# A fused decoder layer on one core: cross k and v and the expert bias from fp32r parts, and score rows stacked one head group at a time

## The chip, the cores and the metric

The kernel runs on 1 core of one Trainium2 chip. The metric is device microseconds (us) from launch to end; lower is better. The core has five engines that run side by side and meet only through semaphores: TensorE (PE in the profile, with its weight loads listed apart as PEld), VectorE (DVE), ScalarE (ACT), GpSimd (POOL) and SyncE (SP), which here only issues DMAs.

## The reference, cut to what matters

Batch B = 8, T = 512 tokens, D = 256. A linear attention with a decaying state comes first, then cross-attention to a context, then a block of self-attention plus a mixture of experts; a layernorm follows each.

```python
# cross-attention: 16 heads of 16
kh = proj(ctx, w_k, b_k); vh = proj(ctx, w_v, b_v); qh = proj(x, w_q, b_q)
out = softmax(qh @ kh.T / 4) @ vh;  x = layernorm(x + out @ w_o.T + b_o)
# third block
qkv = x @ W_qkv + b_qkv                      # self-attention, 16 heads of 16
gate = softmax(x @ W_gate + b_gate)          # 8 experts, the best two kept in `combine`
expert_out = einsum('bsd,edf->bsef', x, W_experts) + b_experts
moe_out = einsum('bsef,bse->bsf', expert_out, combine)
x = layernorm(x + attn_out + moe_out)
```

## The kernel before, in words

**The order is written out by hand.** For each batch n there is a cross phase C n and a self phase S n. They run as C0, C1, S0, C2, S1, ..., C7, S6, S7: 16 phases of 4 head groups (four heads each), and each group takes 4 **slots**, one for each block of 128 keys. So there are 256 slots, and every slot has two halves, h = 0 and h = 1. All engines walk through the same list of halves, t = 2*slot + h, from slot -23 (the prologue) to the end. A table entry such as "kc0": (-14, 0) is a slot and a half, counted from the start of phase C n (for n of 2 and more).

**What PE does in a half.** `scores` (tile sc, two matmuls, one for each side, that is one of the two heads of a pair), `max_tiles` (tile mx, two matmuls that run 6 slots ahead and give the row maxima), in h = 0 also `values` for the slot before (tile op, eight records), and then the **units**, pieces of the other work, nearly all of them in h = 1. A unit writes one of two PSUM banks (`ms`) in turn, and may begin only when the unit two places before it was taken out (`wait_unit_out(pe, *ORDER[u - 2])`). Units that matter here: kc0, kc1, cv0, cv1 (cross k and v from the context), qc0, qc1 (cross q), k3c0 to q3c1 and v3a, v3b (the same of the self phase, already in parts), moe0 to moe15 (experts), combT (the gate weights transposed), be0, be1 (the expert bias), shift (the negated maxima transposed) and heads (the outputs of a group transposed).

**Full precision and parts.** A plain fp32 matmul stands as two records in the trace. Where the operands were cut into a high and a low fp32r part, the product is three fp32r matmuls (high by high, low by high, high by low), one record each (`project_parts`, `project_part_rows`). Before the change kc, cv, be and qc are plain fp32; the self phase and the experts are in parts.

**The other engines.** ACT does one `exps` of 128x1024 in each half, which frees the one sc bank for the next scores, and then its take-outs in the order of the units; DVE does the four row maxima of a slot and its own take-outs; POOL adds expert results and does the small layernorm steps. Each of these engines works strictly in its list's order, and so does SP: `stack` copies the high and low parts of k or q out of `k_parts` or `q_parts` into stacked rows (`ks`, `qs`), and `shift` brings the negated maxima into two more rows of qs.

**Rows and ring.** One `stack` covers two head groups: 6 DMAs of 128 KB, into one of RING = 3 places of 4 tiles. `high` (L698 to L708) may not write the next parts before those DMAs have landed. `max_tiles` waits for the stack of both groups.

**Context.** `ctxT_s` has a buffer of its own; `load_ctx` brings it from HBM. The value tiles v2 hold 20 words for each head (VW = HD + 4), and `values` loads 32 columns from there as weights.

## Time and profile before

| | us |
|---|---|
| median of 3 runs (lowest, highest) | 1268.56 (1268.46, 1268.57) |
| the profiled execution | 1266.94 |
| its span, first to last instruction | 1265.0 |
| PE busy (share of the span) | 1220.8 (96%) |
| DVE busy | 902.8 (71%) |
| ACT busy | 771.1 (61%) |
| POOL busy | 366.0 (29%) |
| mean granted TensorE clock | 0.996 of 2.4 GHz |

How to read it: the 1.94 us between the span and the time of its execution lie outside the instructions. An engine's busy time is the union of its instructions, and matmuls overlap, so that a busy PE says only that something was in flight. How long a piece of PE work really takes is read from starts: from the first scores of one half (tile sc) to the first of the next. In steady flow those halves repeat exactly from batch to batch, so one period stands for all.

### The profile page before, as it was taken

The numbers are of one execution on the slowest core, as the hardware profiler recorded it, in microseconds if no ns is written. First come the engines' busy times: TensorE is split into PE (matmuls) and PEld (weight loads), VectorE is DVE, ScalarE is ACT, GpSimd is POOL, SyncE is SP. The second block draws the span as 40 slices with busy tenths as digits, with TensorE's granted clock in tenths as the row PEclk, the third lists the DMA queues.
The fourth block names the chain that finished last, engine by engine and source line by source line (L and its number), as shares of the span: only waits on it lengthen the run. The fifth ranks groups of instructions, "written<-read, shape, count | busy, mean of one in ns | idle before, by whom it ended". The sixth has DMA issues, their size and how long they took to land.

```text
span 1265.0 us, 19962 instructions
## 1 busy us (share of the span) xinstructions
PE 1220.8 (96%) x6936; PEld 601.8 (48%) x6936; DVE 902.8 (71%) x1836; ACT 771.1 (61%) x1072; POOL 366.0 (29%) x471
## 2 busy tenths in 40 slices
PE   8889999999999999999999999999999999999998
PEld 4433444544555445454554545454454534544443
DVE  2577886677777787777776777767877787667772
ACT  2255556666675765756657665666657576655664
POOL 6410103211621134320522206221153204430261
PEclk9899999999999999999999999999999999999999
DMA  7825034313233342233333143332223333303300
GB/s 254 135 43 94 18 52 68 51 29 76 50 69 52 51 85 42 51 45 70 68 67 61 20 74 68 68 52 45 51 42 51 52 52 52 68 2 52 52 19 18
DMA packets 50243, 74.92 MB, mean 59 GB/s; under 512 B 8536, under 2 KB 20320, under 8 KB 49888
## 3 DMA queue, kind: packets, MB, share of 16 engines
q1 hardware_dynamic: 48896, 72.72, 32.8%
q10 hardware_dynamic: 1248, 0.92, 0.4%
q8 instruction: 57, 0.93, 0.4%
q14 instruction: 42, 0.34, 0.1%
HBM read 18.04 MB, written 4.19 MB: 18 GB/s over the span
## 4 chain that ended last, share of the span: by engine, by line
PE 83%; DVE 7%; ACT 5%; issue 3%; DMA 1%; ACTq 0%; POOL 0%; SPq 0%; DVEq 0%
PE ms L451 38%; PE op L451 17%; PE sc L451 15%; PE mx L451 9%; DVE maxes L928 3%; ACT probs L759 2%; PE ms L557 2%; PE ms L502 1%; ACT moe L752 1%; PE ms L552 1%; DMA qs<-q_parts 1%; DMA w_ident<-in_ident 1%; DVE k_parts L838 0%; ACT x L777 0%; DVE heads L901 0%
## 5 line engine op out<-in xcount | busy, mean ns | idle before, releaser
L928 DVE TENSOR_REDUCE maxes<-mx 128x1 f32<-128x512 f32 x1024 | 657.4, 683 | 215.3 <-PE mx L451 213.4
L759 ACT ACTIVATE probs<-sc 128x1024 f32<-128x1024 f32 x512 | 524.3, 1024 | 373.8 <-PE sc L451 368.3
L1131 POOL TENSOR_TENSOR x<-x,moe 128x256 f32<-128x256 f32 x256 | 187.4, 732 | 687.0 <-ACT moe L752 666.5
L451 PE MATMUL op<-probs,v 128*32 128x512 f32 x2048 | 273.6, 606 | 2.9 <-ACT oT L697 2.5
L451 PE MATMUL sc<-qs,ks 50*128 50x512 f32 x1024 | 256.7, 497 | 11.9 <-ACT probs L759 10.3
L451 PEld LDWEIGHTS sc<-qs,ks 50*128 50x128 f32 x1024 | 95.4, 183 | 308.4 <-ACT probs L759 231.5
L451 PE MATMUL mx<-ks,qs 48*128 48x512 f32 x1024 | 209.0, 402 | 10.9 <-DVE maxes L928 8.9
L752 ACT ACTIVATE moe<-ms,comb 128x256 f32<-128x256 f32 x256 | 106.8, 472 | 22.1 <-PE ms L451 22.1
L451 PEld LDWEIGHTS mx<-ks,qs 48*128 48x128 f32 x1024 | 97.7, 187 | 20.8 <-DVE maxes L928 14.7
L451 PE MATMUL ms<-we_hi,x2T_hi 128*128 128x512 f32 x256 | 93.7, 447 | 2.5 <-DVE shift_r L892 1.3
L451 PEld LDWEIGHTS op<-probs,v 128*32 128x32 f32 x2048 | 40.5, 108 | 96.4 <-issue 95.0
L451 PE MATMUL ms<-we_hi,x2T_lo 128*128 128x512 f32 x256 | 80.5, 396 | 0.0
L451 PE MATMUL ms<-we_lo,x2T_hi 128*128 128x512 f32 x256 | 80.3, 394 | 0.0
L451 PEld LDWEIGHTS ms<-we_hi,x2T_hi 128*128 128x128 f32 x256 | 39.1, 188 | 35.4 <-issue 18.8
L451 PEld LDWEIGHTS ms<-we_lo,x2T_hi 128*128 128x128 f32 x256 | 48.0, 188 | 11.8
L451 PEld LDWEIGHTS ms<-we_hi,x2T_lo 128*128 128x128 f32 x256 | 48.0, 188 | 11.7
L838 DVE SCALAR_TENSOR_TENSOR k_parts<-ms,w_bk,k_parts 128x512 fp32r<-128x512 f32 x32 | 24.0, 751 | 33.7 <-ACT k_parts L698 33.3
L1093 POOL TENSOR_SCALAR var<-mv 128x4 f32<-128x4 f32 x24 | 5.5, 230 | 125.8 <-DVE mv L959 110.7
L557 PE MATMUL ms<-w_ident,oT 128*128 128x128 f32 x256 | 39.9, 279 | 1.8 <-DVE shift_r L892 1.0
L698 ACT ACTIVATE k_parts<-ms,w_bk 128x512 fp32r<-128x512 f32 x32 | 22.0, 687 | 32.1 <-PE ms L451 27.3
L844 DVE TENSOR_TENSOR v<-ms,w_bv 128x512 f32<-128x512 f32 x32 | 22.1, 690 | 27.2 <-PE ms L451 27.2
L557 PEld LDWEIGHTS ms<-w_ident,oT 128*128 128x128 f32 x256 | 29.5, 140 | 20.3 <-DVE shift_r L892 14.5
(131 smaller groups left out, 1264.8 us busy)
## 6 DMA issues: line engine op xcount, KB each, us to landing
ks<-k_parts SPq DMA_DIRECT2D x192, 128.0 KB, 4.2
qs<-q_parts SPq DMA_DIRECT2D x189, 128.0 KB, 4.6
xT_s<-in_xT SPq DMA_DIRECT2D x8, 512.0 KB, 3.8
x_s<-in_x SPq DMA_DIRECT2D x8, 512.0 KB, 4.0
ctxT_s<-in_ctxT SPq DMA_DIRECT2D x8, 512.0 KB, 4.2
out<-x SPq DMA_DIRECT2D x7, 512.0 KB, 2.9
qs<-shift_r SPq DMA_DIRECT2D x128, 8.0 KB
probs<-in_we SPq DMA_DIRECT2D x1, 1024.0 KB, 7.1
```

What stands on the lines that cost most here:

```text
L451: return nc.tensor.matmul(dst, lhsT, rhs, start=first, stop=last, skip_group_check=True)
L502: last = nc.tensor.transpose(bank[:, t * P:(t + 1) * P], src[:, t, c * P:(c + 1) * P], ident[:])
L552: last = nc.tensor.transpose(bank[0:SHIFT * HG * TB, 0:P], shift_n[:, n % 2].rearrange("p s a m -> p (s a m)"), ident[:])
L557: last = nc.tensor.transpose(bank[:, t * P:t * P + P], oT[:, t * P:t * P + P], ident[:])
L698: return nc.scalar.activation(dst, src, ACT.Identity, bias=bias, scale=1.0)
L752: nc.scalar.activation(moe[:, k % 2, j * D:j * D + D], bank[:, j * D:j * D + D], ACT.Copy, scale=comb[:, t, e:e + 1]).then_inc(moe_out, 1)
L759: nc.scalar.activation(probs[:, (2 * s + h) % 3, :, :], sc[:], ACT.Exp).then_inc(exp_out, 1)
L838: nc.vector.scalar_tensor_tensor(out=part[name][:, 1, :].bitcast(F32R), in0=unit_bank((task, n)), scalar=bias[:, c:c + 1], in1=part[name][ ...
L844: return nc.vector.tensor_tensor(dst[:, 2 * h:2 * h + 2, 0:H * VW].rearrange("p n (h d) -> p n h d", h=H)[:, :, :, 0:HD], unit_bank((task, ...
L928: nc.vector.tensor_reduce(maxes[:, g % 2, at:at + 1], mx[:, i % 3, :], AX_X, ALU.max).then_inc(max_out, 1)
L1093: nc.gpsimd.tensor_scalar(var[:, k, :], mv[:, k, :, 1], EPS, None, ALU.add).then_inc(step, 1)
L1131: nc.gpsimd.tensor_tensor(x2[:, n % 2, t, :], x2[:, n % 2, t, :], moe[:, k % 2, j * D:j * D + D], ALU.add).then_inc(acc, 1)
```

## The change

- `kc` and `cv` are made from fp32r parts of the context (`ctxT_part`) and of the weights (`w2_part`), as the self phase already does it. The weights are cut in the prologue (ACT at unit s23, DVE in `first_lows`); of each context ACT cuts the high part (`ctx_high`, two copies of 128x512) and POOL the low one (`ctx_low`, two subtractions; for n = 0 DVE). The context is staged in x1 (n < 2) or x_s, so its load waits for the layernorm that reads x_s, and from n = 3 on the load of x waits for `ctx_low`.
- kc0 and qc0 change places at -14 and -13; for n = 0 and 1 some units move by one slot.
- `stack` covers one group: 6 DMAs of 64 KB into a ring of 5 places of 2 tiles. The second group's rows get a place of their own in SP's list (`second_rows`), and `high` waits for both.
- `be` is one fp32r matmul over 24 rows: combine in high, low and high parts (`comb_parts`, three small DVE instructions) against the bias in high, high and low parts. For n = 1 to 6 combT moves from (33, 1) to (35, 0), between moe1 and q3c0. `above` and `tied` now lie in moe's first buffer, so `choose` waits for the adds of the batch before.
- VW = HD + 1: 17 words for each head.

```diff
 TERMS = 3
 ROWS = TERMS * HD
-VW = HD + 4
+VW = HD + 1
 SHIFT = 2
 SIDES = 2
-PAIRS = H // SIDES
-HALF = PAIRS // DC
-RING = 3
+WIDE = HG // SIDES
+RING = 5
...
-       "o1": (-23, 1), "y01": (-21, 0), "y23": (-20, 0), "x0": (-16, 0), "x1": (-15, 0), "kc0": (-14, 0),
-       "qc0": (-13, 1), "cv0": (-9, 1), "cv1": (-8, 1), "kc1": (-6, 0), "qc1": (-5, 1),
+       "o1": (-23, 1), "y01": (-21, 0), "y23": (-20, 0), "x0": (-16, 0), "x1": (-15, 0), "qc0": (-14, 0),
+       "kc0": (-13, 1), "cv0": (-9, 1), "cv1": (-8, 1), "kc1": (-6, 0), "qc1": (-5, 1),
...
-       "x_bias": (-27, 0), "x1_bias": (7, 0), "load_xT": (-31, 0), "load_x": (-17, 1), "load_ctx": (-1, 0)}
+       "x_bias": (-27, 0), "x1_bias": (7, 0), "load_xT": (-31, 0), "load_x": (-11, 1), "load_ctx": (-17, 1),
+       "ctx_high": (-15, 0), "ctx_low": (-15, 0)}
...
-            "gate": (29, 0), "gateT": (31, 0), "combT": (33, 1), "be0": (36, 0), "be1": (37, 0), "k3c0": (34, 0), "q3c0": (35, 1),
+            "gate": (29, 0), "gateT": (31, 0), "comb_parts": (34, 1), "combT": (35, 0), "be0": (36, 0), "be1": (37, 0), "k3c0": (34, 0), "q3c0": (35, 1),
...
+def second_rows(layer, n, c, kind, soonest):
+    if (layer, n, c) == ("C", 0, 0):
+        return soonest
+    return max(soonest, 2 * (start_of(layer, n) + {"k": (-9, -1), "q": (-8, 0)}[kind][c]))
...
-            for task in ("load_xT", "load_x", "load_ctx"):
+            for task in ("load_xT", "load_x"):
                 halves["sp"][lin_at(task, n)].append((task, n + 1))
+        if n >= 1:
+            halves["sp"][lin_at("load_ctx", n)].append(("load_ctx", n))
+            halves["act"][lin_at("ctx_high", n)].append(("ctx_high", 0, n))
...
-                    halves["sp"][at(f"{name}{c}", n) + 1].append(("stack_" + kind, 2 * PHASE[layer, n] + c))
+                    t, g = at(f"{name}{c}", n), 4 * PHASE[layer, n] + 2 * c
+                    halves["sp"][t + 1].append(("stack_" + kind, g))
+                    halves["sp"][second_rows(layer, n, c, kind, t + 1)].append(("stack_" + kind, g + 1))
...
-        ctxT_s = sb("ctxT_s", [P, DC, T])
+        ctxT_part = (sb("ctxT_hi", [P, DC, T]), sb("ctxT_lo", [P, DC, T]))
+        w2_part = {name: (sb(name + "_hi", [P, DC, D]), sb(name + "_lo", [P, DC, D])) for name in ("wk2", "wv2")}
...
-        combT = o1T[0:E, :]
+        combT = sb("combT", [TERMS * E, T])[:]
...
-        qs = sb("qs", [P, RING, HALF, T])
-        ks = sb("ks", [P, RING, HALF, T])
+        qs = sb("qs", [P, RING, WIDE, T])
+        ks = sb("ks", [P, RING, WIDE, T])
...
+        above, tied = (moe[:, 0, k * TB * E * E:(k + 1) * TB * E * E].rearrange("p (n e f) -> p n e f", n=TB, e=E) for k in range(2))
+        comb3 = sb("comb3", [P, TB, TERMS * E])
+        be_part = sb("be_part", [TERMS * E, D])
+        be_stage = moe[0:TERMS * E, 1, 0:D]
...
+        w2_stage = {name: x1b[:, 2 * k:2 * k + 2, :] for k, name in enumerate(w2_part)}
...
+            return (x1 if n < 2 else x_s)[:].rearrange("p n d -> p (n d)").rearrange("p (c t) -> p c t", c=DC)
...
+                    if n >= 3:
+                        sp.wait_ge(ctx_low, DC * n)
...
+                    if n == 1:
+                        wait_unit(sp, "x0", 0)
+                        wait_unit(sp, "x1", 0)
+                        sp.wait_ge(x1b_out, TB)
+                    elif n >= 2:
+                        sp.wait_ge(ln_out[0], TB * (n + 1))
...
+            def stack(name, g):
                 dst, which = (ks, K_PART) if name == "k" else (qs, Q_PART)
-                sp.wait_ge(part_low[name], e + 1)
-                if e == 0:
+                first = 32 * (g % 2)
+                sp.wait_ge(part_low[name], g // 2 + 1)
+                if g == 0:
                     sp.wait_ge(fills, 5)
-                if e >= RING:
-                    sp.wait_ge(score, 2 * 8 * (e - RING + 1))
-                    sp.wait_ge(max_t, 32 * (e - RING + 1))
-                for side in range(SIDES if (name, e) != ("q", 0) else 1):
+                if g >= RING:
+                    sp.wait_ge(score, 2 * TB * (g - RING + 1))
+                    sp.wait_ge(max_t, HG * TB * (g - RING + 1))
+                for side in range(SIDES if (name, g) != ("q", 0) else 1):
                     for r in range(TERMS):
                         at = 64 * side + HD * r
-                        sp.dma_start(dst[at:at + HD, e % RING, :, :],
-                                     part[name][64 * side:64 * side + 64, which[r], :]).then_inc(stack_in[name], 16)
+                        src = 64 * side + first
+                        sp.dma_start(dst[at:at + HD, g % RING, :, :],
+                                     part[name][src:src + 32, which[r], :]).then_inc(stack_in[name][g % 2], 16)
...
-                    pe.wait_ge(ctx_in, 16 * (n + 1))
-                    last = project(bank, W["wk2"], ctxT_s, slice(c * P, c * P + P))
+                    pe.wait_ge(ctx_low, DC * (n + 1))
+                    if n == 0:
+                        pe.wait_ge(w2_low, 2)
...
-                    last = project_rows(bank, D, ctxT_s, W["wv2"], slice(0, D), (2 * h, 2 * h + 1))
+                    pe.wait_ge(ctx_low, DC * (n + 1))
+                    if n == 0:
+                        pe.wait_ge(w2_low, 2)
...
-                        last = mm(bank[:, j * D:j * D + D], combT[:, t * P:t * P + P], W["be"][:], True, True)
+                        last = mm(bank[:, j * D:j * D + D], combT[:, t * P:t * P + P].bitcast(F32R), be_part[:].bitcast(F32R),
+                                  True, True)
...
+                        pe.wait_ge(stack_in[name][g % 2], 16 * TERMS * SIDES * (g // 2 + 1))
...
+                    for signal in stack_in[name]:
+                        act.wait_ge(signal, 16 * TERMS * SIDES * e)
...
+            def context_high(n):
+                act.wait_ge(ctx_in, 16 * (n + 1))
+                if n >= 1:
+                    wait_unit(act, "kc1", n - 1)
+                    wait_unit(act, "cv1", n - 1)
+                for c in range(DC):
+                    copy(ctxT_part[0][:, c, :].bitcast(F32R), ctx_stage(n)[:, c, :]).then_inc(ctx_high, 1)
...
+                if t == lin_at("s23", 0):
+                    act.wait_ge(w2_in, 16 * 2)
+                    for name in w2_part:
+                        copy(w2_part[name][0][:].bitcast(F32R), w2_stage[name]).then_inc(w2_high, 1)
+                    context_high(0)
...
+                if n >= 1:
+                    dve.wait_ge(acc, 2 * MOE_ENTRIES * n)
+                else:
+                    dve.wait_ge(w3_cut, 4)
...
+            def comb_parts(n):
+                dve.wait_ge(g_step, G_STEPS * n + COMB_STEP)
+                if n >= 1:
+                    wait_unit(dve, "combT", n - 1)
+                nc.vector.tensor_copy(comb3[:, :, 0:E].bitcast(F32R), comb[:]).then_inc(g_step, 1)
+                dve.wait_ge(g_step, G_STEPS * n + COMB_STEP + 1)
+                nc.vector.tensor_tensor(comb3[:, :, E:2 * E].bitcast(F32R), comb[:], comb3[:, :, 0:E],
+                                        ALU.subtract).then_inc(g_step, 1)
+                nc.vector.tensor_copy(comb3[:, :, 2 * E:3 * E].bitcast(F32R), comb3[:, :, 0:E]).then_inc(g_step, 1)
...
+                elif task == "ctx_low":
+                    for c in range(DC):
+                        pool.wait_ge(ctx_high, DC * n + c + 1)
+                        nc.gpsimd.tensor_tensor(ctxT_part[1][:, c, :].bitcast(F32R), ctx_stage(n)[:, c, :], ctxT_part[0][:, c, :],
+                                                ALU.subtract).then_inc(ctx_low, 1)
```

## Rows read from the trace of the kernel before

**Rows 1.** The page's first part: busy time, share of the span, instructions.

```profile
PE 1220.8 (96%) x6936; PEld 601.8 (48%) x6936; DVE 902.8 (71%) x1836; ACT 771.1 (61%) x1072; POOL 366.0 (29%) x471
```

**Rows 2.** The chain that ended last: shares of the span by engine.

```profile
PE 83%; DVE 7%; ACT 5%; issue 3%; DMA 1%; ACTq 0%; POOL 0%; SPq 0%; DVEq 0%
```

**Rows 3.** Stretches: start:end, length, busy of each engine (instructions), clock, DMA; one period.

```profile
439.30:588.60 149.30, 148.45 (x865) 73.71 (x861) 111.75 (x229) 95.91 (x135) 43.43 (x58) 1.00 0.34 58
```

**Rows 4.** Stretches, each one half h = 1, from scores to scores.

```profile
659.27:661.53 2.26, 2.26 (x14) 1.34 (x11) 2.23 (x5) 1.57 (x3) 1.48 (x2) 1.00 1.05 141
...
645.14:648.02 2.88, 2.88 (x21) 1.79 (x17) 1.86 (x4) 1.83 (x3) 0.00 (x0) 1.00 0.00 0
680.64:683.68 3.04, 3.04 (x18) 1.49 (x15) 1.85 (x4) 1.83 (x4) 1.46 (x2) 1.00 0.02 5
685.35:687.92 2.57, 2.57 (x12) 1.05 (x8) 2.51 (x6) 1.02 (x1) 0.00 (x0) 1.00 0.59 133
704.98:708.97 3.99, 3.99 (x23) 2.86 (x19) 2.84 (x7) 1.86 (x3) 0.93 (x2) 1.00 0.00 0
1075.28:1078.97 3.69, 3.69 (x26) 2.92 (x23) 2.17 (x5) 1.03 (x1) 3.69 (x5) 1.00 0.02 4
```

**Rows 5.** PE in order of time, slots 115 to 117: start, us, line, operation, operands, count.

```profile
612.28 0.62 PE L451 MATMUL ms<-we_lo,x2T_hi 128*128 128x512 f32 x2
612.74 0.62 PE L451 MATMUL ms<-x2T_hi,w_hi 128*128 128x512 f32 x2
...
623.40 0.79 PE L451 MATMUL ms<-we_hi,x2T_hi 128*128 128x512 f32 x2
```

**Rows 6.** Stretches: the two halves with a be unit.

```profile
615.90:619.22 3.32, 3.32 (x19) 2.01 (x16) 3.20 (x7) 2.59 (x4) 1.28 (x2) 1.00 0.31 88
620.87:625.06 4.19, 4.19 (x22) 2.37 (x18) 3.07 (x10) 2.17 (x4) 3.88 (x7) 1.00 0.76 87
```

**Rows 7.** ACT in order of time around be1 (slot 117): start, us, line, operation.

```profile
621.42 1.02 ACT L759 ACTIVATE probs<-sc 128x1024 f32<-128x1024 f32 x1
622.75 0.60 ACT L697 ACTIVATE moe<-ms 128x512 f32<-128x512 f32 x1 [0.32 <-PE ms L451]
```

**Rows 8.** Stretches: the halves h = 1 of slots 113, 114 and 115.

```profile
601.09:604.10 3.01, 2.94 (x19) 1.71 (x16) 2.91 (x8) 1.03 (x1) 0.00 (x0) 1.00 0.42 156
605.75:608.93 3.18, 3.02 (x20) 1.94 (x17) 2.04 (x4) 2.27 (x5) 1.46 (x2) 1.00 0.00 0
610.59:614.24 3.65, 3.65 (x22) 2.54 (x18) 2.52 (x6) 1.86 (x3) 1.86 (x2) 1.00 0.55 137
```

**Rows 9.** ACT in order of time: the take-out of moe1 in slot 115.

```profile
612.94 0.84 ACT L752 ACTIVATE moe<-ms,comb 128x256 f32<-128x256 f32 x2 [0.79 <-PE ms L451]
```

**Rows 10.** ACT and then PE in order of time around slot 129, h = 1.

```profile
676.85 1.02 ACT L759 ACTIVATE probs<-sc 128x1024 f32<-128x1024 f32 x1
677.77 0.59 ACT L697 ACTIVATE x1T<-ms 128x512 f32<-128x512 f32 x1
...
678.97 0.50 PE L451 MATMUL sc<-qs,ks 50*128 50x512 f32 x2
```

**Rows 11.** The page's DMA issues: count, KB each, median us to landing.

```profile
ctxT_s<-in_ctxT SPq DMA_DIRECT2D x8, 512.0 KB, 4.2
```

**Rows 12.** SP in order of time: the six DMAs of the first stack of k.

```profile
27.39 3.87 SPq L399 DMA_DIRECT2D ks<-k_parts  x6
```

**Rows 13.** The chain in order of time, in the prologue: start, us, what.

```profile
34.70 8.27 DMA qs<-q_parts
```

**Rows 14.** A stretch of 2 us in the prologue.

```profile
45.00:47.00 2.00, 2.00 (x5) 0.88 (x4) 1.75 (x3) 0.00 (x0) 1.92 (x2) 0.50 1.08 128
```

**Rows 15.** The value tiles' weight loads: duration min/median/max in ns.

```profile
L451 PEld LDWEIGHTS op<-probs,v x2048: 105/108/153, 70.9 to 1254.4; 128*32 128x32 f32 x187
```

**Rows 16.** PE in order of time: one group of values, and the scores behind it.

```profile
619.88 1.06 PE L451 MATMUL op<-probs,v 128*32 128x512 f32 x8
620.87 0.50 PE L451 MATMUL sc<-qs,ks 50*128 50x512 f32 x2
```

More of the change, by code:

```diff
@@ L75 @@
              "stats01": (17, 1), "stats23": (18, 0), "aggr": (18, 0), "root": (18, 0), "apply01": (18, 1),
-             "apply23": (18, 1), "g_exp": (22, 0), "choose": (22, 1), "choose_end": (23, 0)}
+             "apply23": (18, 1), "g_exp": (22, 0), "choose": (22, 1), "choose_end": (23, 0), "comb_parts": (24, 0)}
 LAST = {"sum": (3, 0), "stats01": (4, 0), "stats23": (4, 1), "aggr": (5, 0), "root": (5, 1), "apply01": (7, 0),
@@ L208, in plan_others @@
             halves["dve"][last_at(task, n)].append((task, 2, n))
-        for task in ("choose", "choose_end"):
+        for task in ("choose", "choose_end", "comb_parts"):
             halves["dve"][mid_at(task, n)].append((task, 1, n))
@@ L314, in decoder @@
         w_first, w_in, w_late, we_in = sem("w_first"), sem("w_in"), sem("w_late"), sem("we_in")
+        be_in, be_cut = sem("be_in"), sem("be_cut")
+        w2_in, w2_high, w2_low = sem("w2_in"), sem("w2_high"), sem("w2_low")
+        ctx_high, ctx_low = sem("ctx_high"), sem("ctx_low")
         scaled, we_cut, w3_in, w3_cut, fills = sem("scaled"), sem("we_cut"), sem("w3_in"), sem("w3_cut"), sem("fills")
         x_in, xT_in, ctx_in, y_out = sem("x_in"), sem("xT_in"), sem("ctx_in"), sem("y_out")
-        stack_in = {"k": sem("stack_k_in"), "q": sem("stack_q_in")}
+        stack_in = {name: [sem(f"stack_{name}_in{n}") for n in range(2)] for name in "kq"}
         shift_in = [sem(f"shift_in{n}") for n in range(2)]
@@ L538, in unit @@
                     c = int(task[2])
-                    pe.wait_ge(ctx_in, 16 * (n + 1))
-                    last = project(bank, W["wk2"], ctxT_s, slice(c * P, c * P + P))
+                    pe.wait_ge(ctx_low, DC * (n + 1))
+                    if n == 0:
+                        pe.wait_ge(w2_low, 2)
+                    last = project_parts(bank, w2_part["wk2"], ctxT_part, slice(c * P, c * P + P))
                 elif task in ("qc0", "qc1"):
@@ L547, in unit @@
                     h = int(task[2])
-                    pe.wait_ge(ctx_in, 16 * (n + 1))
-                    last = project_rows(bank, D, ctxT_s, W["wv2"], slice(0, D), (2 * h, 2 * h + 1))
+                    pe.wait_ge(ctx_low, DC * (n + 1))
+                    if n == 0:
+                        pe.wait_ge(w2_low, 2)
+                    last = project_part_rows(bank, D, ctxT_part, w2_part["wv2"], slice(0, D), (2 * h, 2 * h + 1))
                 elif task == "shift":
@@ L735, in take_out @@
                     wait_unit(act, task, n)
-                    copy(combT, bank[0:E, :]).then_inc(done, 1)
+                    copy(combT.bitcast(F32R), bank[0:TERMS * E, :]).then_inc(done, 1)
                 elif task in ("be0", "be1"):
@@ L770, in other @@
                         act.wait_ge(x1b_out, TB * n)
+                    if k == 0 and n < 2:
+                        act.wait_ge(ctx_low, DC * (n + 1))
                     if k == 1 and n == 0:
@@ L778, in other @@
                                              scale=rstd[:, k, t:t + 1]).then_inc(ln_out[k], 1)
+                elif task == "ctx_high":
+                    context_high(n)
                 else:
@@ L1053, in _ @@
                     dve.wait_ge(w3_cut, 4)
+                    dve.wait_ge(be_in, 16)
+                    nc.vector.tensor_copy(be_part[:].bitcast(F32R), be_stage).then_inc(be_cut, 1)
+                    dve.wait_ge(be_cut, 1)
+                    nc.vector.tensor_scalar(be_stage, be_stage, W["side"][:, 0:1], None, ALU.mult).then_inc(be_cut, 1)
+                    dve.wait_ge(be_cut, 2)
+                    nc.vector.scalar_tensor_tensor(out=be_part[:].bitcast(F32R), in0=be_part[:], scalar=W["side"][:, 1:2],
+                                                   in1=be_stage, op0=ALU.mult, op1=ALU.add).then_inc(be_cut, 1)
                 units = UNITS.get(t - 1, [])
@@ L1074, in _ @@
                         choose_end(n)
+                    elif task == "comb_parts":
+                        comb_parts(n)
                     elif k == 2 and n == B - 1:
@@ L1198 @@
         "we": by_chunk(arr(ffn + "W_experts").transpose(1, 0, 2).reshape(D, E * D)),
-        "be": arr(ffn + "b_experts"),
+        "be": np.tile(arr(ffn + "b_experts"), (TERMS, 1)),
+        "side": np.repeat(np.array([[0, 1], [0, 1], [1, -1]], np.float32), E, 0),
         "ident": np.eye(P, dtype=np.float32),
```

89 lines of the change are left out of this document (50 added, 39 removed), and 2 rows, old and new, of the table LIN_FIRST.

## Prediction

> **What bounds the kernel now.** Three views, in this order. The page's first part: PE is busy 1220.8 of 1265.0 us [rows 1], and the chain that ended last runs through PE for 83% of the span [rows 2]. Busy PE may only mean overlapping matmuls, so the next view is stretches. Between slots 80 and 112 one period of two phases takes 149.30 us, of which PE is idle 0.85, and the granted clock is 1.00 [rows 3]; the periods before and after it have the same length. There the order of PE's own work is the time: what a unit loses in length the kernel gains, unless an engine that is less busy turns out to be late. ACT (95.91 of 149.30) and DVE (111.75) have room in sum; whether they have it in a given half has to be asked half by half. The third view is therefore the half itself, from the first scores to the next. The prologue (some 67 us) and the stretches around slots 17 to 31 and 224 to 240 are looser and depend on latency.
>
> **Cross k and v in parts.** A half with one expert unit alone (six fp32r matmuls of 512 columns) takes 2.26 us; one with a plain fp32 projection alone (qc0, four records) 2.57 [rows 4]. kc0 in parts is the first shape, so it saves 0.31. Two parts matmuls start 0.46 us after one another as a pair (612.28 to 612.74) [rows 5], six take 1.4; the rest of the 2.26 is scores, maxima and the switch. kc1 stands between shift and heads: 3.04 us with kc1's like, 2.88 with a parts unit in that place (k3c1) [rows 4], because heads then waits for DVE's take-out of the shift; it saves 0.16. After the swap kc0 is the one that stands alone and qc0 the one beside shift, so kc0 saves the full 0.31. cv0 and cv1 stand beside an expert unit: 3.99 us; with v3b in that place 3.69 [rows 4]; each saves 0.30. The counts: kc0 for n = 2 to 7, 6 x 0.31 = 1.9; kc1, 6 x 0.16 = 1.0; cv, 12 x 0.30 = 3.6; the four units of n = 1, which stand in light halves, 1.2 together. Those of n = 0 lie in the prologue beside a chain through layernorm and q, and count nothing. **Sum 7.7 us.** The Trainium skill (FP8 and Floating Point Precision, TensorE Precision Notes) says that true fp32 takes four passes through the array; by it kc is 8 passes against 6 and a quarter of its 1.7 us would go, 0.43 instead of 0.31, an estimate that would add about 2.6 us over the 22 units that stand free. The rows say 0.31, since a parts matmul takes 0.23 us and not half of 0.43, so the sum goes by them.
>
> **The expert bias.** be0 and moe2 share a half of 3.32 us [rows 6]; without be0 it is 2.26, so be0 costs 1.06. Afterwards it is two fp32r matmuls of 256 columns, half of the 0.46 pair: 0.24. be0 saves 0.82, six times (n = 1 to 6): 4.9. be1 with moe alone (n = 6) saves the same 0.8. For n = 1 to 5 its half holds be1, s0 and moe3 (4.19 us) [rows 6], and moe3 needs the bank that be1 leaves. ACT can take be1 out only behind its exp, which ends at 621.42 + 1.02 = 622.44 [rows 7]; 0.60 later and a hand-over makes 623.07, against 623.40 now [rows 5]. So be1 saves 0.33 and not 0.82: 1.7. n = 0 and n = 7 have the same waits in their halves (0.4 together). **Sum 7.8 us.** The three instructions of `comb_parts` are of 32 columns on DVE, in a half in which DVE is busy 2.04 of 3.18 us [rows 8], and combT comes more than a half later: nothing.
>
> **combT moved behind moe1.** It leaves the half of moe0 (3.01, alone 2.26) and spares the next half its wait for combT's take-out (3.18, the same shape without it 2.88) [rows 4, 8]. That is 1.05, but DVE is busy 2.91 of those 3.01 us [rows 8]: the maxima come late and the next `max_tiles` must wait for a bank; I take 0.73, the bounds are 0.3 and 1.05. In slot 115 the units are now moe1, combT, q3c0, and q3c0 needs moe1's bank. ACT takes moe1 out from 612.94 to 613.78 [rows 9], so q3c0 starts at 613.85 instead of 612.74 [rows 5]: 1.1 lost, with combT's matmuls inside that. **Net loss 0.4 for each of n = 1 to 6: 2.4 us.**
>
> **The context's parts.** POOL's two subtractions and the cut of the weights are hidden: POOL has 106 of 149 us free [rows 3], and kc0 comes three halves after the cut begins. ACT's two copies are not so free. They stand in the first half of slot -15; in the trace that is slot 129, where ACT goes from moe's take-out straight into the exp of the next half at 676.85, which lets PE go on at 678.97 [rows 10]. Queued behind the copies is that exp. A copy of 512 columns takes 0.59 [rows 10], so two put it at 678.0 and its end at 679.0, just past the moment at which PE wants it. I take 0.2 us for n = 3 to 7, **loss 1.0 us**; the bounds are 0 and 0.6 each. The load is the second thing there. Its 4.2 us to landing [rows 11] start after apply23 in slot -17, and SP now has the second group's rows of k ahead of it: six DMAs at 3.87 us of issue [rows 12]. It would be issued at about 671 and land near 675.5, ACT asks for it at 676.8. There is some 1.5 us of cover, and each us beyond it costs five us in all (n = 3 to 7).
>
> **Stack and ring.** The bytes stay the same, SP's issues double: 3.87 us for six [rows 12], so 7.7 for a second group's k and q. SP reaches them right after a shift, they have nothing to wait for there, and the next shift is four slots (about 18 us) away; the rows are needed two slots or more after they land. The ring of 5 groups against the 6 held before is no constraint: group g - 5 has been scored before slot -16 when group g's rows come at -13. Both cost nothing in steady flow; if a shift did come late, PE would wait for it at the first scores of a group.
>
> **The prologue.** The first maxima wait for q's rows, 8.27 us from issue [rows 13], with the DMA engines full; after the change they wait for one group's rows, half the bytes, but SP issues twelve DMAs for k and the next context before them (from 27.4 on [rows 12], 7.7 us and some 0.4 for the context, then three for q until 37.5). That makes the start of the maxima 0 to 2 us sooner. Against it qc1 moves behind the first maxima, where PE runs at the lower of its two levels (0.50, 1.2 GHz, after having stood still for q's rows) [rows 14] and a fp32 projection takes 3.7 instead of 1.7 us. Bounds -2 and +3.6, I take 0.
>
> **Sum.** 7.7 + 7.8 - 2.4 - 1.0 = 12.1 us off the span: 1265.0 becomes 1252.9 and the profiled execution 1266.94 becomes 1254.8. That execution was 1.6 us below the median of the runs, so against 1268.56 the forecast is 1256.5 us.
>
> **VW = 17.** Each value weight load now begins at any multiple of 4 bytes instead of 80. The 2048 loads take 105, 108 and 153 ns at least, in the middle and at most [rows 15], eight of them (0.86) in a group of 0.99 us from 619.88 to 620.87 [rows 16]. So a load may grow by 16 ns before the group does. I take nothing, since the middle and the lowest lie together although heads begin at four different places in 64 bytes. No row shows a start off 16 bytes. The Trainium skill (SBUF — State Buffer, section Door 1: The DMA port swizzle) gives SBUF lines of 16 bytes and a penalty for each new line. 32 words are 8 lines at the old starts and mostly 9 at the new; by that an estimate of 122 ns a load, which would still just fit.
>
> **The rivals.**
> - **The full arithmetic**, 1249.5 to 1252: combT costs nothing net (+2.4), the copies are covered (+1.0), be1 saves more (+0.5 to 1.4), and the prologue gains 1 to 2. For it: ACT idles 0.79 us before moe1's take-out [rows 9]. Against it: that take-out is bound by PE's own end. 18%.
> - **The context comes late**, 1261 to 1265.5: a load that lands 1 to 2 us past ACT's asking stops ACT ahead of an exp, five times, and the clock level in the prologue adds 2 to 3. For it: the DMA engines are near full while rows move (1.05) [rows 4]. Against it: 1.5 us of cover. 14%.
> - **No gain to measure**, 1266 to 1271: DVE or ACT turns out late in most of the shortened halves. DVE is busy 3.20 of 3.32 us in be0's half [rows 6], which is to become 2.50. Against it: the halves around it leave DVE idle, and 37 us in a period. 6%.
> - **Slower by the value weights.** Mechanism: the weight loads of `values` at starts off 16 bytes. The price is 8 x 256 = 2048 loads, so 2.05 us for each ns beyond the 16 of cover; the 12.1 us are gone at 22 ns more a load, and at 30 ns more the time is 1256.5 + 28.7 = 1285. For it: the loads already fill 87% of the group. Against it: the flat durations. 7%.
>
> **How the numbers follow.** The forecast's own case, 1253 to 1260.5, has 55%. The range takes in the full arithmetic and most of the late context: 1249.5 to 1264. About 0.2% (2.5 us) is what a measurement of this kernel can tell from no change. Faster than that: 55 + 18 + 14 = 0.87; within it 0.06; slower 0.07.
>
> **What would show it.** The period of 149.30 should become about 147.4; halves with cv and moe 3.69, with kc0 alone 2.26, with be0 and moe 2.50, with moe1, combT and q3c0 about 4.8 with a wait for ACT's moe, and a short wait for the exp after slot -15. The value loads should stay at 108 ns. The prediction is wrong if those loads grow, if PE's scores wait for a DMA of the shift, or if ACT stands before `ctx_high` waiting for the context.

## The result and the profile after

The changed kernel takes 1263.53 us in the median of six runs (1262.27 to 1264.17), the kernel before 1268.57 beside it: a ratio of 0.9963, interval 0.9947 to 0.9979. It is 5.0 us faster where 12.1 were forecast. Run again beside others (e10 below) it gave 1264.96 against 1268.89, 0.9966 [0.9949, 0.9983]. The profiled execution took 1263.36 with a span of 1261.6, so 3.4 us of span are to be explained here; 8.7 of the 12.1 forecast are missing.

The page's first part, the answer to [rows 1] (line 451 of before is 480 now, 928 is 982, 759 is 796):

```profile
PE 1208.0 (96%) x7000; PEld 603.5 (48%) x7000; DVE 915.9 (73%) x1867; ACT 780.2 (62%) x1090; POOL 381.7 (30%) x485
```

PE's busy time fell by 12.8 us and the span by 3.4: its work did shrink, and its idle time rose from 44.2 to 53.6 us. The same period as in [rows 3], from slot 80 to slot 112 (length, busy of PE, PEld, DVE, ACT, POOL, clock, DMA share, GB/s):

```profile
444.70:592.96 148.26, 146.80 (x870) 73.71 (x870) 113.31 (x231) 96.93 (x137) 45.97 (x60) 1.00 0.24 59
```

A period fell from 149.30 to 148.26, not to 147.4, and PE's idle part in it rose from 0.85 to 1.46. Half by half, in the same view as [rows 4, 6, 8]:

```profile
600.61:602.96 2.35, 2.35 (x14) 1.42 (x10) 2.25 (x7) 1.02 (x1) 0.00 (x0) 1.00 0.68 214
602.96:605.13 2.17, 1.94 (x14) 0.56 (x13) 2.03 (x5) 1.62 (x3) 0.16 (x1) 1.00 0.05 18
605.13:608.01 2.88, 2.88 (x20) 1.84 (x16) 2.19 (x5) 1.57 (x3) 1.32 (x2) 1.00 0.00 0
609.68:614.76 5.08, 4.59 (x25) 2.84 (x21) 2.77 (x6) 2.32 (x4) 3.21 (x3) 1.00 0.34 77
616.42:619.34 2.92, 2.77 (x16) 1.64 (x12) 2.80 (x6) 2.49 (x4) 0.73 (x1) 1.00 0.10 22
621.01:624.72 3.71, 3.71 (x19) 1.94 (x16) 2.92 (x10) 2.06 (x4) 3.40 (x7) 1.00 0.18 41
684.99:687.26 2.27, 2.27 (x15) 1.43 (x12) 2.24 (x6) 1.03 (x1) 0.00 (x0) 1.00 0.33 74
704.32:708.00 3.68, 3.68 (x26) 2.91 (x22) 2.83 (x7) 1.87 (x3) 0.74 (x1) 1.00 0.46 109
718.93:721.83 2.90, 2.90 (x21) 1.79 (x17) 1.88 (x4) 2.90 (x6) 1.48 (x2) 1.00 0.00 0
```

In order: slot 113 without combT (3.01 before), slot 114's first half (1.65 before), its second (3.18), slot 115 with moe1, combT and q3c0 (3.65), be0 and moe2 (3.32), be1, s0 and moe3 (4.19), kc0 alone (2.57), moe13 and cv0 (3.99), shift, kc1 and heads (3.04). The last three are where the forecast put them. The fourth is the loss, and there the waits can be read in order of time (start, length, engine, operation, count, idle before it and its releaser):

```profile
608.98 0.18 DVE L1121 CAST comb<-comb 128x32 fp32r<-128x32 f32 x1
...
609.39 1.28 DVE L982 TENSOR_REDUCE maxes<-mx 128x1 f32<-128x512 f32 x2
...
610.12 0.19 PEld L480 LDWEIGHTS mx<-ks,qs 48*128 48x128 f32 x2 [0.26 <-DVE maxes L982]
...
612.07 0.60 PE L627 MATMUL ms<-w_ident,comb 128*24 128x128 f32 x4
612.26 0.84 ACT L789 ACTIVATE moe<-ms,comb 128x256 f32<-128x256 f32 x2 [1.03 <-PE ms L480]
612.99 0.57 ACT L731 ACTIVATE combT<-ms 24x512 fp32r<-24x512 f32 x1
...
613.16 0.73 PE L480 MATMUL ms<-x2T_hi,w_hi 128*128 128x512 f32 x2 [0.49 <-ACT moe L789]
```

q3c0 waits for moe1's bank, as foretold, and the half had already begun late: `comb_parts` (three instructions from 608.98) stands on DVE ahead of the maxima, for which PE's weight load then waits 0.26. The waits of PE from 60 us to the end (total, times, longest; the first line is of before, the others of after) say how often such things happen:

```profile
PE mx L451 <- DVE maxes L928: 5.8, 9, 1.2
...
PE mx L480 <- DVE maxes L982: 7.8, 17, 1.0
PE ms L480 <- ACT moe L789: 3.2, 7, 0.5
...
PE ms L480 <- DVE q_parts L892: 2.1, 8, 0.6
```

Waits for maxima rose from 5.8 us in 9 places to 7.8 in 17; the other two are 0.49 for moe1 and 0.15 for q3c0's take-out, six times each, beside a few single ones.

**The ledger**, from the starts of all halves in both traces, span against span (forecast in brackets): prologue +1.75 (0); kc and cv -8.05 (-7.7); combT with its parts +5.9 (+2.4); be units -5.3 (-7.8); slots 29 and 30, where the granted clock fell, +2.4 (0); the context's copies +0.1 (+1.0). Together -3.2 of the 3.4. The clock's term is a difference to e1 below, which has the same code in slots 29 and 30 and no fall of the clock there: 15.87 us in the changed kernel, 13.48 in e1.

### The profile page after: what moved, and what is told of

Read it like the earlier page. It is cut to its first block, busy times and chain, and to the rows that moved or that the text cites. A ratio compares the mean times of both kernels' runs of the same rounds, so it can differ in the third digit from the quotient of the medians.

```text
span 1261.6 us, 20667 instructions
## 1 busy us (share of the span) xinstructions
PE 1208.0 (96%) x7000; PEld 603.5 (48%) x7000; DVE 915.9 (73%) x1867; ACT 780.2 (62%) x1090; POOL 381.7 (30%) x485
## 3 DMA queue, kind: packets, MB, share of 16 engines
HBM read 18.06 MB, written 4.19 MB: 18 GB/s over the span
## 4 chain that ended last, share of the span: by engine, by line
PE 79%; DVE 9%; ACT 5%; issue 3%; DMA 1%; SPq 1%; POOL 0%; ACTq 0%; DVEq 0%
PE ms L480 34%; PE op L480 16%; PE sc L480 15%; PE mx L480 9%; DVE maxes L982 5%; PE ms L590 2%; ACT probs L796 2%; PE ms L531 2%; SPq L427 1%; ACT moe L789 1%; PE ms L585 1%; DMA w_ident<-in_ident 1%; DVE q_parts L892 0%; ACT q_parts L732 0%; DMA qs<-q_parts 0%
## 5 line engine op out<-in xcount | busy, mean ns | idle before, releaser
L480 PE MATMUL sc<-qs,ks 50*128 50x512 f32 x1024 | 257.3, 498 | 12.4 <-ACT probs L796 11.4
L731 ACT ACTIVATE oT<-op 128x512 f32<-128x512 f32 x64 | 38.4, 600 | 1.4 <-PE op L480 1.4
```

The source lines that it names most:

```text
L480: return nc.tensor.matmul(dst, lhsT, rhs, start=first, stop=last, skip_group_check=True)
L731: return nc.scalar.activation(dst, src, ACT.Copy)
```

## The experiments

Times are compared with the kernel before on the same chip: 1268.95 for the first four runs, 1267.57 for the next four, 1268.89 for the last three.

**e5: the expert bias as before.** combT of 8 rows stands in slot 33 again, the be units are plain float32, `comb_parts` is gone.

```
-            "gate": ..., "comb_parts": (34, 1), "combT": (35, 0), ...
+            "gate": ..., "combT": (33, 1), ...
-                        last = mm(bank[...], combT[:, ...].bitcast(F32R), be_part[:].bitcast(F32R), True, True)
+                        last = mm(bank[...], combT[0:E, ...], be_part[0:E, :], True, True)
...
```

> The changed kernel with the expert bias as it was before: combT of 8 rows at (33, 1), be0 and be1 plain fp32, no comb_parts. Only cross k and v, ring and value width remain changed. Theory A (the bias part of the change lost through the order of the banks what its matmuls gained): the halves of slots 33 to 36 return to 3.01, 1.66, 3.18, 3.65 and 3.32 us, kc and cv halves keep their gain (about 8 us in all), the prologue keeps its loss of 1.75; the time is 1262 to 1263, so the whole bias part was worth about nothing (0 to +1 us). Rival B (the bias part did bring most of its forecast 5 us and something else ate the gain): 1267 or more.

Measured: 1263.64, ratio 0.9961 [0.9940, 0.9982]. The halves of slots 113 to 117 are back at 3.22 (3.00 to 3.02 in the same place of four other elements, as before the change), 1.66, 3.17, 3.66, 3.32 and 4.18. So the whole bias part of the change, forecast at 5.4 us net, is worth nothing that can be measured.

**e2: combT back beside moe0**, products still in parts.

```
-"comb_parts": (34, 1), "combT": (35, 0)
+"comb_parts": (33, 0), "combT": (33, 1)
```

> The changed kernel with combT back at (33, 1) and comb_parts at (33, 0), the bias still in parts. Theory A: q3c0 no longer waits for ACT's take-out of moe1 in slot 35, whose half falls from 5.08 to 3.65, and be0's half from 2.92 to 2.50; against it DVE does comb_parts just before combT, so slot 33 takes 3.5 to 3.7 instead of 2.35 and slot 34's second half 3.2 instead of 2.88. The five halves fall from 15.4 to about 14.9, 0.5 x 6 = 3 us: 1260 to 1261. Rival B (DVE is the bound around slots 33 to 36): the five halves stay at 15.4 or more, 1263.5 or more.

Measured: 1262.51, 0.9948 [0.9923, 0.9972]. Slot 115 is back at 3.66 (5.08), so the place and the parts cost 1.42 there; but slot 113 went to 3.55, since PE now waits for DVE's parts. The transposes in order of time:

```profile
602.42 0.60 PE L627 MATMUL ms<-w_ident,comb 128*24 128x128 f32 x4 [0.60 <-DVE comb L1125]
```

A period is 147.7 (148.2 in the changed kernel). be0's half stayed at 2.91 where 2.50 was expected, so its shortfall is not from combT's place; the time, too, missed the 1260 to 1261 expected.

**e1: combT, be0 and be1 in later slots** (elements 1 to 6), so that moe1 and q3c0 follow one another again and be1 stands beside o1.

```
-"combT": (35, 0), "be0": (36, 0), "be1": (37, 0)
+"combT": (36, 0), "be0": (37, 0), "be1": (41, 0)
```

> The changed kernel with combT at (36, 0) beside moe2, be0 at (37, 0) beside s0 and moe3, be1 at (41, 0) beside o1. Theory A: slot 35 falls from 5.08 to 3.65, slot 36 is 3.01 (combT and moe2), slot 37 stays near 3.7, slot 41 grows from 3.02 to 3.3; 1.1 x 6 = 6 us: 1257 to 1258.5. Rival B (the loss lies with DVE or ACT being full there, not with the order of the banks): the loss moves to slots 36 and 37 and the time stays within 2 us of 1263.5.

Measured: 1258.03, 0.9923 [0.9892, 0.9954]. Slot 115's half is 3.87: combT in it had cost 1.21, and the 0.22 over 3.65 belong to `comb_parts`, for with the parts elsewhere (e2) it is 3.66. The half that held o1 alone (3.02) holds be1 too and takes 3.46. Its be unit on PE:

```profile
634.62 0.50 PE L480 MATMUL ms<-be_part,combT 24*128 24x256 f32 x2
635.05 2.42 PE L480 MATMUL ms<-lin 128*128 128x512 f32 x8
```

From the start of the pair to the next unit are 0.43 us, not the 0.24 of the sum. Slot 116 with combT and moe2 is 2.92, the same as with be0 and moe2. By the halves the new places are worth 1.21 less 0.44 in each of six elements, 4.6 us; the profile also has no fall of the clock at slot 29, and one at slot 238, of which the last section tells.

**e3: the value tiles 17 wide**, the only edit, on the kernel before.

```
-VW = HD + 4
+VW = HD + 1
```

> The kernel before with VW = HD + 1 alone. Theory A: value weight loads that begin off 16 bytes cost the same 108 ns, the time stays 1268.5 within 0.1%. Rival B: they cost more, hidden in the changed kernel by other gains; the median load would be 110 or more and the time above 1270.

Measured: 1267.08, 0.9993 [0.9963, 1.0024]: no difference. Weight loads of the values (min/median/max ns):

```profile
L451 PEld LDWEIGHTS op<-probs,v x2048: 105/107/111, 70.3 to 1251.8; 128*32 128x32 f32 x187
```

**e8: kc and cv plain float32 again**, on the changed kernel.

```
-                    last = project_parts(bank, w2_part["wk2"], ctxT_part, slice(c * P, c * P + P))
+                    last = project(bank, w2_part["wk2"][0], ctxT_part[0], slice(c * P, c * P + P))
...
-                    last = project_part_rows(bank, D, ctxT_part, w2_part["wv2"], slice(0, D), (2 * h, 2 * h + 1))
+                    last = project_rows(bank, D, ctxT_part[0], w2_part["wv2"][0], slice(0, D), (2 * h, 2 * h + 1))
...
```

> The changed kernel with one part undone: the context's k and v projections (kc0, kc1, cv0, cv1) are plain float32 matmuls again, two of 512 columns in place of six in fp32r; the high copies are whole copies, the low parts are still written and not read, and everything else (ring of five, context stage, stack order, expert bias in parts) stays. Theory A (this part alone carries the steady gain, 1.2 us per element from n = 2 on and 8.0 us in all, as the halves of the two traces differ): the time comes out 6.5 to 9 us above the changed kernel, 1270 to 1272.5 against a changed kernel of 1263.5, so no faster than the kernel before; kc0 alone is 2.57 us again, moe+cv 3.99, shift+kc1+heads 3.04. Rival B (the gain of these halves comes from the new places of the row copies and of the context's loading, and would be there without fp32r): the time stays within 2 us of the changed kernel, and the three halves stay at 2.26, 3.68 and 2.89.

Measured: 1269.85, 1.0018 [0.9989, 1.0046]. kc0's half is 2.59, moe with cv 3.99, shift with kc1 3.04, and the half of x2T0 and qc1 went from 3.17 to 3.34 too. kc0 in order of time, four records in place of six:

```profile
687.27 1.98 PE L480 MATMUL ms<-ctxT_hi,wk_hi 128*128 128x512 f32 x4
689.19 0.50 PE L480 MATMUL sc<-qs,ks 50*128 50x512 f32 x2
```

So this part carries the whole gain of the change; without it the kernel is no faster than before.

**e4: in the prologue, q's first group ahead of k's second.**

```
-        return soonest
+        return lin_at("qc0", 0) + 2
...
-"load_ctx": (-15, 0),
+"load_ctx": (-14, 1),
```

> The changed kernel with one edit in the prologue: of element 0 the row copies of the second groups (k and q) are issued behind those of the first groups, from two halves after qc0, and the context of element 1 is loaded one half later. Theory A (slot 0 starts 1.75 us later than in the kernel before because SyncE issues twelve k copies, 8.5 us, before the first q copy): the first row maxima start 3 to 5 us before 43.75 and slot 0 starts 1.5 to 4 us earlier, 65 to 67 us in place of 68.60; the time comes out 1.5 to 4 us under the changed kernel. Rival B (the prologue is bound by VectorE's maxima and the projections at the lower clock, not by the copies): slot 0 starts within 0.7 us of 68.60 and the time moves by less than 1 us.

Measured: 1263.26, 0.9971 [0.9945, 0.9998], and slot 0 at 68.03 in place of 68.60. The first maxima did come 5.2 us sooner:

```profile
38.51 0.49 PE L480 MATMUL mx<-ks,qs 48*128 48x512 f32 x2
...
40.36 0.69 ACT L732 ACTIVATE k_parts<-ms,w_bk 128x512 fp32r<-128x512 f32 x1 [8.21 <-DMA ks<-k_parts]
...
41.08 0.75 DVE L892 SCALAR_TENSOR_TENSOR k_parts<-ms,w_bk,k_parts 128x512 fp32r<-128x512 f32 x1 [5.30 <-ACT k_parts L732]
41.74 2.56 DVE L982 TENSOR_REDUCE maxes<-mx 128x1 f32<-128x512 f32 x4
...
42.48 0.49 PE L480 MATMUL mx<-ks,qs 48*128 48x512 f32 x2 [3.47 <-DVE maxes L982]
```

But kc1's take-out on ACT must wait until k's copies have read the buffer. Moved back, they free it at 40.36 (38.26 before the edit), DVE's part of the take-out waits for ACT, and the first reduction stands behind it on DVE. The wait for q's rows had only become another, so the forecast of 1.5 to 4 us was wrong. The rival's numbers came out, but not its whole reason: a copy of rows still stands in the chain. This profile also has a fall of the granted clock to 0.50 between 60 and 64 us, which the changed kernel's has not; what it hid of the gain is not shown.

**e6: element 2's last normalisation half a slot later.**

```
-"apply23": (-20, 1)
+"apply23": (-19, 0)
```

> The changed kernel with one edit: the normalisation of the last two row blocks of element 2's first layer (apply23 on ScalarE) runs one half later, from slot -20 second half to slot -19 first half of its schedule, so that ScalarE is free to take the attention output out at slot 29 sooner. Theory A (TensorE stands still 1.66 us there because ScalarE is busy with the apply, and the granted clock then falls to 0.50 for some 6 us, which costs 2 us in slots 29 and 30): the wait at slot 29 shrinks to under 0.8 us, the clock stays at 1.0, slot 29's second half goes from 5.53 to 3.5 to 4.1 us, and the time falls by 2 to 3 us. Rival B (the clock's fall there doesn't hang on this wait, as the kernel before has the same wait and no fall): the wait shrinks, the gain is 0.5 to 1 us and the second half of slot 29 stays over 5 us in the profile.

Measured: 1261.74, 0.9951 [0.9928, 0.9974], 1.8 us under 1263.53 where 2 to 3 were expected. The intervals of the two ratios overlap, so the gain in time is not shown by itself; the halves are. Slot 29 in the changed kernel, PE in order of time and two stretches:

```profile
202.56 1.24 PE L480 MATMUL op<-probs,v 128*32 128x512 f32 x8 [1.66 <-ACT oT L731]
...
203.00:206.00 3.00, 3.00 (x16) 1.40 (x9) 1.02 (x2) 1.60 (x3) 0.00 (x0) 0.55 0.74 183
206.00:209.00 3.00, 3.00 (x10) 2.13 (x8) 1.64 (x3) 0.94 (x2) 1.27 (x1) 0.50 0.08 29
```

The same place with the edit:

```profile
203.31 1.07 PE L480 MATMUL op<-probs,v 128*32 128x512 f32 x8 [0.68 <-ACT oT L731]
...
204.00:207.00 3.00, 2.56 (x16) 1.47 (x13) 1.78 (x4) 2.94 (x6) 0.42 (x1) 1.00 0.56 98
```

The wait is 1.0 shorter, the clock holds, and the second half of slot 29 takes 3.79 instead of 5.53.

**e7: e1 and e6 together, and be1 of elements 0 and 7 a slot later.**

```
-"be0": (29, 0), "be1": (30, 0)
+"be0": (29, 0), "be1": (31, 0)
```

> The changed kernel with three edits at once: combT and the bias products move to slots with room (combT 36, be0 37, be1 41, for the elements 1 to 6), be1 of the elements 0 and 7 goes from slot 30 to 31, and element 2's apply23 runs one half later. Expected from the parts: the move gave 5.5 us of median when run alone (1263.5 to 1258.0), be1 in slot 31 takes back 0.6 us in element 7's half where shift, be1 and heads met (3.53 to 2.89) and as much lies at element 0, the apply up to 1 us beyond the clock that the move already held: 1255.5 to 1257.5. If instead the halves that receive the work are full (the theory that no half of the middle has room, every product costs its whole length wherever it stands), the time is that of the changed kernel, 1262 to 1264.

Measured: 1255.84, 0.9903 [0.9869, 0.9937]. Element 7's half with shift and heads went from 3.53 (4.00 in e1) to 1.97, for 0.47 more in the half that now holds be1. Element 0 paid: -0.4 in slot 30, but +1.2 in slot 31 and +1.5 in slot 32, where PE waits for an exp that stands behind two late take-outs:

```profile
222.30 0.49 PE L480 MATMUL sc<-qs,ks 50*128 50x512 f32 x2 [1.47 <-ACT probs L796]
```

**e10: the changed kernel, unaltered, beside the two below.**

> The changed kernel once more, unaltered, beside the two kernels below on one chip, so that they can be compared with it. If its 1263.5 us stands for it, the median comes out between 1262 and 1265, 0.994 to 0.998 of the kernel before. A rival reading of its gain (the six executions happened to be good ones) would give 1266 or more.

Measured: 1264.96 (1260.93 to 1270.80). Its profile is used in the two parts below.

**e12: e7, with be1 later for element 7 only.**

```
     slot, half = (MID_SHORT if n in (0, B - 1) else MID_LONG)[task]
+    if (task, n) == ("be1", B - 1):
+        slot += 1
```

> The kernel with three edits (combT and the bias products moved to slots 36, 37 and 41; element 2's apply23 one half later; be1 one slot later), but be1 is now one slot later for element 7 alone. Theory A (the halves are independent: at element 0 the later be1 costs 1.2 us in slot 31's second half and 1.5 us in slot 32's, where the scores then wait 1.47 us for the exp, and takes 0.4 us off slot 30; at element 7 it gains 2.6 us): element 0's halves go back to 4.7, 3.7 and 2.3 us, element 7's stay at 1.97, 1.67 and 2.73, the time is 1.5 to 2.5 us under the kernel with be1 later for both, 1253.5 to 1254.5. Rival B (the late exp at slot 32 is of another cause, such as the normalisation's new place): the half of slot 32 stays at 3.8 us and the time at 1255 to 1257.

Measured: 1253.55 (1253.13 to 1254.64), 0.9888 [0.9873, 0.9902]. Slots 30 to 32 are back at 4.71, 3.70 and 2.26, element 7's stay at 1.96, 1.66 and 2.74: the halves did act independently. The page's first part, and the period (slot 80 to 112):

```profile
PE 1202.9 (96%) x7000; PEld 601.3 (48%) x7000; DVE 922.2 (74%) x1867; ACT 779.8 (62%) x1090; POOL 381.8 (31%) x485
...
440.97:588.63 147.66, 146.67 (x870) 73.66 (x870) 114.29 (x230) 96.97 (x136) 45.98 (x60) 1.00 0.24 59
```

This beats both kernels, by 15.3 and 11.4 us (four executions).

**e9: e12 with e4's edit.**

> The same kernel with a fourth edit: of element 0 the row copies of the second groups stand behind those of the first, as in the run in which this was done alone. There the first maxima started 5.2 us sooner and slot 0 only 0.6 us sooner, because ScalarE's take-out of kc1 then waited for the moved k copies (40.36 in place of 38.26) and VectorE's first maxima stood behind it. Theory A (that wait has taken the place of the one removed): slot 0 starts within 0.7 us of 68.0 again and the time is within 1 us of the kernel without the edit. Rival B (the gain was there and a fall of the granted clock at 60 to 64 us hid it): without such a fall slot 0 starts 1.5 to 3 us sooner, at 65 to 66.5, and the time falls by as much.

Measured: 1254.18, 0.9892 [0.9879, 0.9905]; slot 0 at 69.42 (68.69 in e12), later than theory A's 68.7 at most, with the time within its 1 us. As in e4, the granted clock fell once more between 59 and 67 us (0.79), so rival B's condition, no such fall, did not arise and it stays open; what speaks for theory A is that the first pair of maxima starts at 39.11 and the second at 43.08, after a wait of 3.47 us for DVE, as in e4.

## Why the prediction was right and wrong

In short: the forecast was right on what bounds the kernel and wrong in the terms of the bias. A be unit was priced at 0.24 us and takes 0.43; moe2's wait behind be0 was left out; moving combT was to bring 0.73 and brought 0.44; and `comb_parts`, put at nothing, costs 0.22 for each element. The prologue's +1.75, taken as 0, and the clock at slot 29 come on top.

**What bounds the kernel: right.** PE's order is the time in steady flow, and every half that lost PE work without meeting another wait lost it in the span.

**Cross k and v in parts: right**, -8.05 against -7.7. kc0 gave 0.30 to 0.33, cv 0.31 and 0.29, kc1 0.14. That the sum came out so near is partly luck, for two things that it left out cancel. Each half of x2T0 and qc1 fell by 0.16, 0.9 in all: qc1 starts 0.06 after DVE has taken out heads, in both traces (726.27 and 726.33 before, 724.69 and 724.75 after), and that comes sooner behind the shorter kc1 (e8 takes it back when kc and cv alone are undone). And the half with element 1's cv1, slot 4, grew from 2.98 to 3.26 in place of losing 0.30: DVE cuts the bias into `be_part` just ahead of the maxima there, and PE waits 0.32 for them; in e5, where one plain copy stands for that cut, the half is 2.68. The estimate of 0.43 for kc0, worked out from the Trainium skill (FP8 and Floating Point Precision, TensorE Precision Notes), did not come: 0.30. A plain matmul is two records of 0.43 here, 0.86; a quarter of that is 0.21, and an fp32r matmul takes 0.23.

**The expert bias, 7.8 forecast, 5.3 measured.** The term that was mis-sized is the price of a be unit after the change. It was put at half of a running pair of 512 columns, 0.24; alone between other units it takes 0.43 to 0.44 (e1 beside o1; 2.69 with moe6 against 2.26). In cv the 256-column pairs do follow at 0.24 (3.68 less 2.26 is six times that), so the columns are not what costs. The trace of before had the same 0.2 in it; PE in order of time:

```profile
616.57 1.13 PE L451 MATMUL ms<-w_be,o1T 8*128 8x256 f32 x4
617.62 0.73 PE L451 MATMUL ms<-we_hi,x2T_hi 128*128 128x512 f32 x2
```

be0 took 1.05 us to the next unit, where four records of half of 0.43 make 0.86, an estimate. The change took away the difference of the columns, 0.62, and left the 0.2, which the forecast had let go with them. A plain projection between the tiles of scores and maxima has it as well (kc0 in e8: 1.92 for four of 0.43), and a cv right behind a moe has it not. So it goes with the neighbours of a unit, not with plain or parts. be's operands are 24 rows high, between units of 128; whether that change or the exposed weight load makes the 0.2 was not separated.

The second miss is be0's half: 0.62 was to be had even so, 0.40 came, because moe2 needs the bank of q3c0, and DVE's take-out of that ends at 617.69:

```profile
616.94 0.75 DVE L892 SCALAR_TENSOR_TENSOR q_parts<-ms,bq3s,q_parts 128x512 fp32r<-128x512 f32 x1
...
617.75 0.73 PE L480 MATMUL ms<-we_hi,x2T_hi 128*128 128x512 f32 x2 [0.15 <-DVE q_parts L892]
```

The same 2.91 stands when combT is in be0's place (e1, e12). The no-gain rival had this condition, DVE late in be0's half, and it held there, though not in most halves. be1 gave 0.48 where 0.33 was taken. Element 7 lost 0.5, since be1 in a half with shift and heads makes heads wait 0.92 for the shift's take-out; elements 0 and 7 together had been put at a gain of 0.4.

**combT moved: right in kind, wrong in size.** Out of slots 113 and 114 it was to bring 0.73 and brought 0.44 (3.01 to 2.35, 1.65 to 2.17, 3.18 to 2.88): DVE is later against the shortened half than assumed, within the bounds given. Behind moe1 it was to cost 1.1 and costs 1.21. And "`comb_parts` costs nothing" was wrong: 0.22 for each element (e1 and e2 against each other), because the three small instructions stand ahead of the maxima on DVE. A busy share of 2.04 of 3.18 us said that there was room in the half, not at that point of it. Per element +0.99 instead of +0.4. How the 0.22 arises is read from the order and the one wait of 0.26; no run changed it alone.

**The context's parts: the forecast loss of 1.0 did not come in this execution, but the cover was thinner than forecast.** The load is issued at 670.46 and ACT does not wait for it. ACT and PE's weight load in order of time:

```profile
676.48 1.16 ACT L731 ACTIVATE ctxT_hi<-x_s 128x512 fp32r<-128x512 f32 x2
677.52 1.03 ACT L796 ACTIVATE probs<-sc 128x1024 f32<-128x1024 f32 x1
...
678.62 0.19 PEld L480 LDWEIGHTS sc<-qs,ks 50*128 50x128 f32 x2 [0.36 <-ACT probs L796]
```

The exp ends at 678.55, 0.07 before PE starts its scores. The step that failed by a tenth was the length of the copies: back to back they hold ACT for 1.04 us (676.48 to 677.52), not for twice the 0.59 of [rows 10]. The 1.5 us of cover for the load are another matter. In e10, the same program, it was issued at 677.09, and ACT stood before the copies in slot 129:

```profile
682.38 1.16 ACT L731 ACTIVATE ctxT_hi<-x_s 128x512 fp32r<-128x512 f32 x2 [0.36 <-DMA x_s<-in_ctxT]
```

That is 5.3 us from issue to landing, not 4.2, and the half took 3.11 in place of 2.65. In six of the eleven profiles with the new load (e1, e4, e5, e7, e9, e10) ACT waits so once or twice, 0.36 to 0.70 each, and the half is 0.45 to 0.79 longer. So the prediction's own sign of being wrong, ACT standing before `ctx_high`, does occur. The time lies in the range of the rival "the context comes late", and its mechanism is real, but it strikes one or two halves in place of five and does not make the 8.7 us: the profile that the ledger is from has none of it.

**Stack and ring: right**, no wait of PE for rows or shift stands in the steady part. **VW = 17: right**; the loads stay at 108 ns here and 107 in e3. The estimate of 122 ns worked out from the Trainium skill (SBUF — State Buffer, Door 1: The DMA port swizzle) does not come true, and the rival of 7% is refuted.

**The prologue: +1.75 within its bounds of -2 and +3.6, taken as 0.** The rows' smaller size did not make them sooner. Twelve k copies took 8.47 us of issue, q's own followed at 36.71, and the maxima waited 5.06 us until 43.75, 0.6 later than before. And qc1, which had run ahead of them in 1.98 us, now runs behind them at 1.2 GHz (granted clock 0.50) in 3.78. PE before (two lines) and after (two lines):

```profile
38.68 1.98 PE L451 MATMUL ms<-x1T,w_wq 128*128 128x512 f32 x4
43.11 0.50 PE L451 MATMUL mx<-ks,qs 48*128 48x512 f32 x2 [2.01 <-DMA qs<-q_parts]
...
43.75 0.79 PE L480 MATMUL mx<-ks,qs 48*128 48x512 f32 x2 [5.06 <-DMA qs<-q_parts]
46.02 3.78 PE L480 MATMUL ms<-x1T,w_wq 128*128 128x512 f32 x4
```

That the maxima would start 0 to 2 us sooner was wrong: q's copies were issued 1.2 us later than the 35.5 that the forecast's issue times add up to. The slow qc1 it had in its upper bound. How the 1.75 divides between the two was not measured. In the eight profiled executions with this prologue (after, e1, e2, e5, e6, e7, e10, e12) slot 0 starts between 68.01 and 75.59, against 66.85 and 66.19 in two with the old one.

**What no step had foreseen** is the clock in slots 29 and 30, 2.4 us in the profiled execution.

So of the 8.7 us missing, 3.5 are in combT and its parts, 2.5 in the be units, 2.4 in the clock at slot 29 and 1.75 in the prologue; 1.25 come back from kc, cv and the context, and 0.2 is what the ledger leaves over.

## What to carry to other kernels

Price a unit by a half that holds it, not by half of a running pair of larger ones (the old half held the extra 0.2, and making the columns cheaper did not take it away), and count what small instructions of another engine stand in front of at their point of the order, not the share of time in which that engine is free. A product that got cheaper is worth only what its neighbours let through: here the bias part gained nothing where it stood, and the same products in other slots (e1) made the median 5.5 us shorter. When a wait is moved out of a prologue, ask which buffer the moved copies hold.

## What the runs showed of the hardware

Executions of one program differ by several us with the granted clock, and the place can be read. The changed kernel's prologue, in the profile of after and of e10, the same program (stretch, length, busy times, clock, DMA share, GB/s):

```profile
37.00:43.00 6.00, 1.70 (x5) 0.57 (x4) 0.75 (x1) 4.74 (x4) 0.38 (x1) 0.99 0.87 169
43.00:51.00 8.00, 6.18 (x12) 2.56 (x12) 2.86 (x5) 2.17 (x5) 7.92 (x2) 0.58 0.48 127
51.00:59.00 8.00, 5.97 (x20) 2.67 (x20) 7.16 (x12) 1.83 (x4) 8.00 (x8) 1.00 0.35 67
```

and e10:

```profile
43.00:51.00 8.00, 6.88 (x12) 2.74 (x12) 2.62 (x5) 2.71 (x5) 7.92 (x2) 0.50 0.46 125
51.00:59.00 8.00, 6.51 (x12) 2.71 (x12) 4.28 (x7) 1.37 (x3) 8.00 (x8) 0.50 0.30 69
59.00:67.00 8.00, 7.22 (x16) 3.51 (x15) 5.48 (x11) 0.00 (x0) 1.54 (x2) 0.50 0.12 47
```

In both PE had waited for q's rows (5.06 and 4.52 us) and came back at the lower level, 1.2 GHz. In one it was at 2.4 GHz again by 51 us, in the other it stayed down over PE's busy stretches to 67 us, and slot 0 starts 7.0 us later. At slot 29 the wait of 1.66 us was followed by a fall in after, e2, e4, e5 and e10, and by none in before, e1, e3 and e8 with the same wait. With the wait at 0.66 to 0.69 (e6, e7, e12, e9) no profile shows one. A second such place is slot 238 of element 7, where heads waits 0.92 for the shift's take-out: within 2 us of it the clock fell to 0.50 in e1, e2, e4, e6 and e10, and not in after or e8 with the same units there; with be1 a slot later (e7, e9, e12) it fell in none. In e1 the halves of slots 238 and 239 took 1.5 us more for it than in after. That a shorter wait helps rests on these profiles and on e6's 1.8 us; what decides in a single execution is open. In the kernel before, runs of 1264.4, 1268.9 and 1277.5 us have mean granted clocks of 0.999, 0.995 and 0.985.
